# Four transposes of the probabilities, spread over the first projection of each unit step

## The reference, cut to what matters

```python
q = (x @ wq).reshape(B, S, N_Q_HEADS, HEAD_DIM)
k = (x @ wk).reshape(B, S, N_KV_HEADS, HEAD_DIM)
v = (x @ wv).reshape(B, S, N_KV_HEADS, HEAD_DIM)
q = _rope(q, pos)
k = _rope(k, pos)
qg = q.reshape(B, S, N_KV_HEADS, G, HEAD_DIM)
scores = jnp.einsum('bqhgd,bshd->bhgqs', qg, k) * sm_scale
...
allowed = (j <= i) & (j > i - SLIDING_WINDOW)
scores = jnp.where(allowed[None, None, None], scores, neg)
attn = jax.nn.softmax(scores, axis=-1)
out = jnp.einsum('bhgqs,bshd->bqhgd', attn, v).reshape(B, S, N_Q_HEADS * HEAD_DIM)
return out @ wo
```

## Time and profile before

| | us |
|---|---|
| median of 3 runs | 1562.42 (1562.02 to 1563.08) |
| span of the profiled execution | 1564.6 |
| PE busy | 1510.8 (97%) |
| DVE busy | 1143.0 (73%) |
| ACT busy | 923.4 (59%) |
| POOL busy | 868.2 (55%) |
| chain that ended last | PE 65%, DVE 11%, issue 10%, POOL 6%, ACT 5% |

### The profile page before, as it was taken

How to read it: one execution, slowest core, us unless ns; L and a number is a source line. 1 busy time by engine, 2 the same in 40 slices (tenths; PEclk the granted TensorE clock), 3 DMA queues, 4 the chain that set the end, 5 groups by cost and what they waited for, 6 DMA issues and landing times.

```text
span 1564.6 us, 27263 instructions
## 1 busy us (share of the span) xinstructions
PE 1510.8 (97%) x7561; PEld 1247.8 (80%) x7561; DVE 1143.0 (73%) x1809; ACT 923.4 (59%) x2323; POOL 868.2 (55%) x892
## 2 busy tenths in 40 slices
PE   7999999999999999978999999999999999988998
PEld 3478888888888888866788888888888888867887
DVE  5587787878777878787787868787878778775432
ACT  4575666666666666565665656565657666654431
POOL 1356465655555646566665655555565656674422
PEclk9899999999999999999999999999999999999999
DMA  8210101101010101022310202020201011131001
GB/s 282 62 48 21 47 20 33 34 27 40 27 40 27 40 27 40 7 74 61 101 42 9 59 0 60 7 60 7 60 7 47 20 47 34 34 102 34 28 28 54
DMA packets 75083, 70.28 MB, mean 45 GB/s; under 512 B 4888, under 2 KB 54048, under 8 KB 75040
## 3 DMA queue, kind: packets, MB, share of 16 engines
q1 hardware_dynamic: 73328, 65.55, 13.8%
q10 hardware_dynamic: 1072, 2.10, 0.4%
q0 software_dynamic: 640, 2.10, 0.3%
HBM read 63.45 MB, written 6.29 MB: 45 GB/s over the span
## 4 chain that ended last, share of the span: by engine, by line
PE 65%; DVE 11%; issue 10%; POOL 6%; ACT 5%; DMA 1%; DVEq 0%; ACTq 0%; POOLq 0%; SPq 0%
PE pP L269 8%; PE pP L271 8%; PE pP L270 8%; PE pOp L269 6%; PE pOp L271 6%; PE pOp L270 6%; PE pS L269 3%; PE pS L271 3%; PE pS L270 3%; POOL pm L1222 3%; PE pAv L269 3%; PE pAv L270 3%; PE pAv L271 3%; PE pTr L279 3%; DVE wp L992 2%
## 5 line engine op out<-in xcount | busy, mean ns | idle before, releaser
L1222 POOL TENSOR_SCALAR_AFFINE_SELECT pm<-pT 128x512 fp32r<-128x512 f32 x480 | 390.4, 846 | 500.1 <-DVE pT L859 500.1
L269 PE MATMUL pP<-hT,wp 128*128 128x512 f32 x768 | 313.6, 408 | 2.6 <-ACT rB L635 1.5
L271 PE MATMUL pP<-hT,wp 128*128 128x512 f32 x768 | 302.4, 394 | 0.0
L270 PE MATMUL pP<-hT,wp 128*128 128x512 f32 x768 | 301.1, 392 | 0.0
L624 ACT ACTIVATE pr<-pr,nb 128x128 f32<-128x128 f32 x512 | 199.7, 393 | 82.3 <-DVE nb L874 79.9
L1235 POOL TENSOR_TENSOR rB<-rB,tab 128x512 f32<-128x512 f32 x160 | 224.5, 1415 | 30.3 <-ACT rB L635 30.1
L269 PE MATMUL pOp<-wos,oT 128*128 128x512 f32 x512 | 203.8, 398 | 11.9 <-DVE oT L854 10.9
L270 PE MATMUL pOp<-wos,oT 128*128 128x512 f32 x512 | 202.4, 395 | 0.0
L271 PE MATMUL pOp<-wos,oT 128*128 128x512 f32 x512 | 202.3, 395 | 0.0
L884 DVE TENSOR_TENSOR rA<-pP,tab 128x512 f32<-128x512 f32 x160 | 110.1, 689 | 121.6 <-ACT rB L635 121.6
L617 ACT COPY pr<-pS 128x512 f32<-128x512 f32 x128 | 75.0, 586 | 171.4 <-PE pS L271 170.6
(11 more groups left out here) (174 smaller groups left out, 3155.6 us busy)
## 6 DMA issues: line engine op xcount, KB each, us to landing
st<-in_L_attn_wq_dram SPq DMA_DIRECT2D x64, 256.0 KB, 3.8
st<-in_L_attn_wo_dram SPq DMA_DIRECT2D x64, 256.0 KB, 2.8
xin<-in_L_attn_x_dram SPq DMA_DIRECT2D x32, 256.0 KB, 3.0
st<-in_L_attn_wk_dram SPq DMA_DIRECT2D x16, 256.0 KB, 2.6
wm<-in_L_wmod_dram SPq DMA_DIRECT2D x4, 1024.0 KB, 9.0
st<-in_L_attn_wv_dram SPq DMA_DIRECT2D x16, 256.0 KB, 2.7
out_dram<-st SPq DMA_DIRECT2D x16, 256.0 KB, 2.0
st<-in_L_ffn_w_dram SPq DMA_DIRECT2D x12, 256.0 KB, 3.3
```

Of the source, the lines that this page charges most:

```text
L269: nc.tensor.matmul(o, hi_l, hi_r, start=start, stop=False, skip_group_check=True)
L270: nc.tensor.matmul(o, hi_l, lo_r, start=False, stop=False, skip_group_check=True)
L271: return nc.tensor.matmul(o, lo_l, hi_r, start=False, stop=stop, skip_group_check=True)
L1222: last = nc.gpsimd.affine_select(out=pm[:, own, part], in_=pT[:, part], compare_op=op, fill=0.0, base=0, pattern=[[0, G], [sign, P]], chan ...
```

## The change

Inside the hardware loop, the four transposes of unit u-1 no longer stand as a block behind `p_times_v`. One is issued behind each of the four groups of three matmuls of the step's first projection. The waits for them stand ahead of the first one. Outside the loop nothing changes. Only PE's program is touched.

```diff
+            def trans_head(f, u, h):
+
+                if h == 0:
+                    f.wait(u_norm, PER_U, u + 1)
+                    f.wait(u_phi, PER_U, u)
+                    f.wait(u_plo, PER_U, u)
+                done = nc.tensor.transpose(pTr[:, h * P:(h + 1) * P], pr[:, u % 2, h, :], ident[:])
+                if h == G - 1:
+                    done.then_inc(u_trans, 1)
+
             def trans(f, u):
-
-                f.wait(u_norm, PER_U, u + 1)
-                f.wait(u_phi, PER_U, u)
-                f.wait(u_plo, PER_U, u)
                 for h in range(G):
-                    last = nc.tensor.transpose(pTr[:, h * P:(h + 1) * P], pr[:, u % 2, h, :], ident[:])
-                last.then_inc(u_trans, 1)
+                    trans_head(f, u, h)
...
-                last.then_inc(j_pe, 1)
+                    if k == KT - 1:
+                        last.then_inc(j_pe, 1)
+                    if woven:
+                        woven(k)
...
-                if prev:
+                if prev and not weave:
                     trans(f, u - 1)
...
-                        unit_step(f, u, b, lambda: slot_jobs(f, u, b), lambda: slot_late(f, u, b))
+                        unit_step(f, u, b, lambda: slot_jobs(f, u, b, lambda k: trans_head(f, u - 1, k)),
+                                  lambda: slot_late(f, u, b), weave=True)
```

More of the change, by code:

```diff
@@ L328, in bank_free, with project @@
                     f.wait(r_cos, PER_R, r)
-            def project(f, name, ch, j, w, r=None):
+            def project(f, name, ch, j, w, r=None, woven=None):
                 bank_free(f, PER_J, j, r)
@@ L389, in filler, with slot_jobs @@
                     ln_transpose(4 + i)
-            def slot_jobs(f, u, b):
+            def slot_jobs(f, u, b, woven=None):
                 js, second = u // NT, u % NT >= CH
@@ L397, in slot_jobs @@
                             10 * (js + second) + SLOT[name] + 1,
-                            PER_R * js + (10 if second else 5) + SLOT[name] - 1 if SLOT[name] >= 2 else None)
+                            PER_R * js + (10 if second else 5) + SLOT[name] - 1 if SLOT[name] >= 2 else None,
+                            woven if name == JOBS_OF_U[u % CH][0] else None)
             def slot_late(f, u, b):
@@ L404, in slot_late, with unit_step @@
                     turn_v(f, jbase(b) + (6 if second else 0) + PER_J * js + SLOT["V"])
-            def unit_step(f, u, b, jobs, late=lambda: None, prev=True, prev2=True):
+            def unit_step(f, u, b, jobs, late=lambda: None, prev=True, prev2=True, weave=False):
                 scores(f, u, b)
```

## The result

The changed kernel takes 1680.0 us (median of 4 runs, 1676.7 to 1689.3) against 1562.4 (4 runs, 1562.0 to 1563.1): a ratio of 1.0757, 95% interval 1.0737 to 1.0777. The forecast was 1680, with a range of 1640 to 1712.

What follows compares the result with a forecast made beforehand. PE, busy 97% of the span, sets the pace, with the mask and Q3's rope_lo last behind it. 1564.6 + 99 (stalls) + 18 (clock) = 1681.6 us, the profiled execution lying 2.2 above the median: 1680, range 1640 to 1712.

Steps and rivals of the forecast that it cites:

- the late release: Fourth transpose in the loop: u_trans comes 2.79 us later, and what queues in order behind p_hi and p_lo moves with it.
- Some of its signs: Profile after: PE busy below 92%; waits of 1.5 us for the mask, 0.9 for result_lo, 1.6 for v_copy.
- steps 3 and 7, scores behind Q3's rope_lo: End of steps 3 and 7: Q3's rope_lo ends later, so the next scores start 2.35 us later, twice a turn.
- step 5 into 6, the mask: p_times_v of step 6 waits for the later mask: 1.33 us a turn.
- step 1 into 2, result_lo: DVE's step 1 runs late, merge and result_lo follow, out_proj of step 2 starts 0.92 us later a turn.
- lone transposes in the other steps: Steps 0, 4 and 6: four transposes standing singly cost 0.04 us more a step, 0.12 a turn; other engines' work fits.
- the clock, both loops: Standstills ending steps 3 and 7 drop PE's clock at two places in five of 28: 18 us, between 0 and 44.
- Clock up throughout: Rival: the stalls come as counted and the clock stays up, 1661 us; chance 0.2.
- Falls at all 28 places: Rival: the stalls come and the clock falls at every one of the 28 places, 1705 us; chance 0.17.
- Engines parted by the shift: Rival: rope_lo and mask run shorter once shifted apart, 67 us of stalls, 1629 without clock losses; chance 0.1.
- More waits than counted: Rival: a wait held to be covered, such as normalise, opens too, say 1 us a step, over 1715; chance 0.06.
- Faster and no effect: Rivals: transposes vanish between pP matmuls, 1513 us, chance 0.02; or engines catch up, 4 us or nothing, chance 0.03.

Runs made afterwards that it cites:

- e5: Changed kernel with the four transposes as a block again in the loop, behind the 12 matmuls of the first projection: 1681.4 us, ratio 1.0754.
- e6: Changed kernel with one transpose behind each of the first four matmuls of the projection instead of behind each third: 1572.9 us, ratio 1.0057.
- e9: Changed kernel with ACT taking the exponentials ahead of p_hi and DVE the rope sums ahead of p_lo, PE's program unchanged: 1603.1 us, ratio 1.0248.
- e8: Changed kernel with six extra matmuls of 512 columns, result unused, ahead of turn_v in the loop: 1664.5 us, ratio 1.0642.
- e4: Changed kernel with the transposes woven only in steps 0, 2, 4 and 6, the block elsewhere: 1573.3 us, ratio 1.0059.
- e2: Changed kernel with the transposes woven only in step 5, the block elsewhere: 1579.7 us, ratio 1.0111.
- e1: Changed kernel with the transposes woven only in steps 3 and 7, the block everywhere else: 1651.4 us, ratio 1.0561.
- e7: Kernel before, with the four transposes woven among the last matmuls of p_times_v: 1566.6 us, ratio 1.0017.
- e11: Changed kernel with twelve extra transposes of 128 columns, result unused, ahead of turn_v in the loop: 1665.9 us, ratio 1.0659.
- e3: Changed kernel with the transposes woven only in step 1, the block elsewhere: 1579.8 us, ratio 1.0101.
- e12: Changed kernel with only two extra matmuls of 512 columns, result unused, ahead of turn_v in the loop: 1666.8 us, ratio 1.0662.

## Why the prediction was right

**The mechanism held**: the late release, shown by e5 (late without weaving, 1681) and e6 (woven, the fourth transpose 0.95 us later by its sum instead of 2.79, 1573), and its path through the in-order queues by e9. In step 3 `p_hi` comes 2.77 us later (forecast 2.79), `p_lo` 2.31 and the end of `rope_lo` 2.32 (forecast 2.35 for both). The waits stand where the prediction puts them. Some of its signs were a little off: PE is busy for 92.2%, not below 92; PE stands 1.2 us for the mask, not 1.5, and 0.70 for `result_lo`, not 0.9.

**Its terms**, in us a turn, against what was measured:

| place | forecast | measured |
|---|---|---|
| steps 3 and 7, scores behind Q3's rope_lo | 2.35 each | 2.32 and 2.33 |
| step 5 into 6, the mask | 1.33 | 1.42 (0.38 + 1.04) |
| step 1 into 2, result_lo | 0.92 | 1.06 |
| lone transposes in the other steps | 0.12 (steps 0, 4 and 6) | 0.14 (steps 4, 0 and 1; that of step 6 is in the mask's row) |
| both loops together | 99 | 98.6 (e8) |
| the clock, both loops | 18 (0 to 44) | 17.8 |

Two sizes were off, and small. The slack of steps 4 to 5 was put at enough: "Steps 0, 4, 6 hold two projections, and the work of the other engines fits". It doesn't in step 4, e4 shows 0.37 a turn in step 5 for it; in the changed kernel this lies inside the wait for the mask, so it costs next to nothing there (steps 5 and 6 lose 1.42 together, and 1.36 in e2, where step 4 is not woven). In step 2 the release of `out_proj` was costed at 0.13 behind `result_lo`; it is 448.06 - 447.84 = 0.22, that is 0.09 more, of the 0.14 by which step 2 comes out longer than I had it. The price of the lone transposes, 0.04 a step, is that of e5 against the changed kernel: 0.04 and 0.06.

**The clock term** came out by luck as much as by reading. Two places in five of 28 were a choice between rows; 10 places, one of them double, is that number, but e1, with the same standstills at the same 28 places, has 15, and e5 has 11. The four runs of the changed kernel scatter over 12.6 us, those of e8, which has no falls in its loops, over 3.6; but the twelve of e7, which has none either, scatter over 7.9, so the scatter is the clock's only in part. The level of this term is known to some 10 us either way, not better.

The 2.2 us that the sum takes off mix two measures: a profiled span is not the time of its execution (1679.1 and 1680.66 in the changed kernel). Nothing hangs on it, as 1562.4 + 99 + 18 is 1679.4.

**The rivals.** Clock up throughout (1661) is what e8 shows: 1664.5. Falls at all 28 places (1705) are excluded by the changed kernel itself, which has 10, and the ground for them, that transposes do not count, by e11. Engines parted by the shift: here they were not, 3.99 in the earlier trace rows and 3.99 after; but where an experiment did part them (e9), the mask took 3.15, so the effect is real. More waits than counted: the one for `normalise` opens in e3, for 4.3 us in all, and not in the changed kernel (0.3 us). Faster and no effect are excluded by the result.

## What to carry to other kernels

Weaving small operations between large ones on TensorE is worth nothing if each has its price anyway (here 0.11 to 0.12 us for a transpose, in a block or alone), and it moves the release of the last one back by the length of all that it is woven into. Before moving an instruction on an engine that is busy all the time, look at the others' in-order queues: what stands behind the instruction that waits for it, and how much room has the release that comes last (here the `rope_lo` of Q3, with none). The same reading shows the gain that is there: two operations moved ahead of the merge in one step of DVE, which is busy for 73% only, took 0.4% off a kernel that looked bound by TensorE.

## What was not expected of the hardware

- Standstills of TensorE of 1.56 + 0.29 us, with four transposes between, were followed by a fall of the clock at 10 to 15 of 28 places (changed kernel, e1, e5); of 1.03 us, at one of 28 (e12). In one execution of the changed kernel the falls differ from loop to loop, with the same instructions: 1 in the first and 9 in the second.
- Twelve transposes of 128x128 in float32 kept the clock at 1.00 as six matmuls of 512 columns did (e11, e8).
- Extra matmuls whose result nobody uses made the kernel 15.6 us faster (e8; 16.9 against e5 on the same chip).
- Four mask instructions on POOL took from 2.39 (e9, step 4) to 4.00 us (changed kernel, step 5), by what DVE did beside them: 0.88 to 0.89 for one beside `rope_sum`, 0.63 to 0.64 for one beside `rope_cos` (kernel before).
